# One decoder layer on one core: the time mix part begun inside the last cross attention rounds

## The reference

```python
# 1. self attention with sigmoid instead of softmax
qn, kn = layer_norm(x @ Wq.T + bq), layer_norm(x @ Wk.T + bk)
attn = sigmoid(qn @ kn.T / sqrt(256) - log(1024))
x = layernorm(x + ((attn @ v) @ Wo.T + bo) * layerscale)
# 2. cross attention, 16 heads of 16, over the 77 context tokens
attn = softmax(qh @ kh.T / 4)
x = layernorm(x + (attn @ vh) @ dense_w.T + dense_b)
# 3. time mix (x_prev is x one token earlier in its sequence)
xr, xk = mu_r * x + (1 - mu_r) * x_prev, mu_k * x + (1 - mu_k) * x_prev
out = sigmoid(xr @ W_r.T) * (relu(xk @ W_k.T) ** 2 @ W_v.T)
x = layernorm(x + out)
```

## Time and profile before

| what | value |
|---|---|
| median of three runs | 612.66 us |
| profiled execution, its own time | 616.14 us |
| its span, first to last instruction | 614.3 us |
| mean granted TensorE clock | 0.945 of full speed |
| busy, share of the span: PE / PEld / DVE / ACT / POOL | 88% / 79% / 73% / 76% / 58% |
| ACT_TABLE_LOAD of ScalarE, 1283 ns each | 60 |

### The profile page before, as it was taken

One profiled execution on the slowest core, in us unless ns is written; L12 is line 12 of the kernel. 1 busy time (PEld: TensorE's weight loads), 2 busy tenths in 40 slices (PEclk: granted clock), 3 DMA queues, 4 the chain that ended last, 5 costly groups with the idle time before them and its releaser, 6 DMA issues.

```text
span 614.3 us, 12601 instructions
## 1 busy us (share of the span) xinstructions
PE 537.6 (88%) x4526; PEld 484.4 (79%) x4526; DVE 448.8 (73%) x981; ACT 465.3 (76%) x1109; POOL 358.6 (58%) x498
## 2 busy tenths in 40 slices
PE   7979899899898989898998998898896664699993
PEld 5769898797888879797888887797785444699993
DVE  4775668878779697878788795667664534589995
ACT  2644389797888888887978889988984525799984
POOL 2763547666666575757656664653744531059996
PEclk9999999999999999999999999999997566899998
DMA  6421210101010101101010101102013000001112
GB/s 160 136 72 14 44 35 1 36 1 35 2 53 1 52 2 53 36 19 52 1 37 2 36 1 36 36 1 87 2 37 136 1 2 0 1 18 54 52 52 103
DMA packets 28850, 23.01 MB, mean 37 GB/s; under 512 B 7412, under 2 KB 28788, under 8 KB 28788
## 3 DMA queue, kind: packets, MB, share of 16 engines
q1 hardware_dynamic: 28084, 21.55, 11.5%
q10 hardware_dynamic: 704, 0.66, 0.5%
HBM read 15.07 MB, written 6.82 MB: 36 GB/s over the span
## 4 chain that ended last, share of the span: by engine, by line
PE 30%; DVE 20%; POOL 17%; issue 15%; ACT 13%; DMA 2%; SPq 1%; POOLq 0%; DVEq 0%; ACTq 0%
PE st L257 7%; PE xb L257 6%; POOL p_sb L763 5%; DVE qk_sb L919 5%; PE xb L1366 4%; DVE st L1042 4%; PE proj L257 4%; ACT p_sb L515 4%; PE xb L1350 3%; POOL fold L758 3%; POOL vv_lo L707 2%; POOL xs L751 2%; PE acc L257 2%; POOL rs L698 2%; PE proj L1248 1%
## 5 line engine op out<-in xcount | busy, mean ns | idle before, releaser
L515 ACT ACTIVATE p_sb<-xb,neg_mx 128x77 f32<-128x77 f32 x512 | 114.2, 375 | 19.0 <-DVE neg_mx L981 18.7
L763 POOL TENSOR_TENSOR p_sb<-p_sb,rc 128x1280 f32<-128x1280 f32 x32 | 79.1, 2471 | 74.3 <-DVE rc L994 74.3
L257 PE MATMUL st<-qkT_hi 128*128 128x256 f32 x256 | 76.9, 300 | 0.0
L257 PE MATMUL acc<-vv_hi,aT_hi 128*128 128x256 f32 x256 | 75.3, 294 | 0.0
L257 PE MATMUL st<-qkT_lo,qkT_hi 128*128 128x256 f32 x256 | 72.8, 284 | 0.0
L257 PE MATMUL st<-qkT_hi,qkT_lo 128*128 128x256 f32 x256 | 72.8, 284 | 0.0
L257 PE MATMUL acc<-vv_lo,aT_hi 128*128 128x256 f32 x256 | 72.3, 283 | 0.0
L257 PE MATMUL acc<-vv_hi,aT_lo 128*128 128x256 f32 x256 | 72.3, 283 | 0.0
L1350 PE MATMUL xb<-ident,p_sb 128*128 128x128 f32 x320 | 53.2, 295 | 18.3 <-ACT p_sb L515 13.1
L981 DVE TENSOR_REDUCE neg_mx<-xb 128x4 f32<-128x308 f32 x128 | 52.2, 470 | 18.4 <-PE xb L1337 18.3
L758 POOL TENSOR_TENSOR fold<-p_sb 128x640 f32<-128x640 f32 x32 | 50.7, 1583 | 25.8 <-ACT p_sb L515 25.6
(11 more groups left out here) (201 smaller groups left out, 1750.6 us busy)
## 6 DMA issues: line engine op xcount, KB each, us to landing
xraw<-in_xT SPq DMA_DIRECT2D x16, 256.0 KB, 3.1
xs<-in_x SPq DMA_DIRECT2D x16, 256.0 KB, 3.0
out_y<-y SPq DMA_DIRECT2D x16, 256.0 KB, 2.1
x_kept<-xs SPq DMA_DIRECT2D x10, 256.0 KB, 2.2
x2s<-x_kept SPq DMA_DIRECT2D x5, 512.0 KB, 5.6
cT<-in_cT SPq DMA_DIRECT2D x1, 308.0 KB, 3.3
wraw<-in_wqT ACTq DMA_DIRECT2D x2, 128.0 KB, 3.5
wraw<-in_wkT SPq DMA_DIRECT2D x2, 128.0 KB, 3.7
```

The source lines that it names most:

```text
L257: mm = pe.matmul(out, s_, m_, start=first and k == 0 and q == 0, stop=last and k == n - 1 and q == 2, skip_group_check=not check)
L515: ex = act.activation(weights(t)[:, h // KH * (H // 2) + KH * n + h % KH, 0:SC], logits[n][:, h * SC:(h + 1) * SC], ACT.Exp, bias=neg_mx[: ...
L763: pool.tensor_tensor(weights(t), weights(t), rc[:, t % 2].rearrange("p (h o) -> p h o", o=1) .to_broadcast([P, H, SP]), ALU.mult).then_inc ...
```

## The change

It has five parts.

1. Every engine's order is new. The prologue is written out step by step and reaches further (self attention scores up to number 4 and the first query stand in it); the rounds are 16 with other order inside; everything from there to the end is written out, with steps of the time mix part among the last cross attention steps. `exponentials` and `maxima` are called for one bank of heads at a time, `qk_stats` is cut in `qk_bias` and `qk_stats`, `wf_split` in three.
2. The first five pairs (ND) of the time mix part use the four banks that self attention leaves free; from pair 5 on the banks alternate with those of cross attention.
3. The mixtures are written to SBUF (`xm`) and read there by `mix_hi` and `mix_lo`.
4. The norm of q and k is two tensor_tensor over 512 columns (times scale, then plus bias, both broadcast along the row), the second waiting for the first.
5. The buffers of the time mix part lie where those of the parts before are free earlier; the loads of its weights and of the kept rows are issued earlier.

```diff
-NR_ALL = NJ + 5
+ND = 5
-        xm_bank, fr_bank, fk_bank, fv_bank = st_bank, cross_bank[0], cross_bank[1], [cross_bank[2], cross_bank[3]]
+        def in_turn(own, cross):
+            return lambda i: own if i < ND or (i - ND) % 2 else cross
+        ty_bank, fv_bank = in_turn(proj[:], cross_bank[0]), in_turn(acc_ps[:], cross_bank[2])
+        fr_bank, fk_bank = in_turn(st_bank[0], cross_bank[1]), in_turn(st_bank[1], cross_bank[3])
+        def same_bank(i):
+            return i - 1 if i < ND else i - 2
...
+            xm = tensor(ph, "xm", [P, 2, 2, BANK])
...
             @block.sync
                 def load_again(n):
...
+                    w.wait_ge(*(av_pe.at(4 * (NJ - JB) - 1) if n < JB else st_pe.at(LAST)))
...
-                w.wait_ge(*av_pe.at(LAST))
             @block.scalar
+                    w.wait_ge(*mx_dve.at(t, n + 1))
+                    for h in range(HG):
...
                 def key_relu(i):
                     w.wait_ge(*fk_pe.at(i))
+                    w.wait_ge(*av_pe.at(LAST))
...
+                def round_(r):
+                    at(norm2, r - 5)
+                    at(exponentials, 2 * r - 4, NT, 0, 0)
+                    at(exponentials, 2 * r - 4, NT, 0, 1)
+                    at(exponentials, 2 * r - 4, NT, 0, 2)
+                    at(tqk_hi, 2 * r + 7, NT, 11)
...
+                exponentials(30, 3)
+                weights_tail(29)
+                key_relu(0)
+                carried(2)
+                mixed_hi(14)
+                key_squares(0)
+                exponentials(31, 0)
...
             @block.gpsimd
                 def round_(r):
+                    at(fold_weights, 2 * r - 6, NT)
+                    at(xt_lo, r + 4, NJ, 6)
+                    at(qk_deviation, 2 * r + 6, NT, 11)
+                    at(normalise, 2 * r - 6, NT)
+                    at(deviation1, r - 2, NJ, 1)
+                    at(deviation2, r - 5)
+                    at(fold_weights, 2 * r - 5, NT)
+                    at(residual2, r - 2, NJ, 1)
+                    at(qk_deviation, 2 * r + 7, NT, 11)
+                    at(normalise, 2 * r - 5, NT)
+                    at(v_lo, r + 3, NJ, 6)
+                    at(residual1, r - 1, NJ, 2)
...
             @block.vector
                 def qk_norm(i):
...
+                    both = tiles(qk_sb[:, i % 4])
+                    scale, bias = (t[:, i % 4].rearrange("p (m o) -> p m o", o=1).to_broadcast([P, 2, D]) for t in (rs1, nb1))
+                    dve.tensor_tensor(both, both, scale, ALU.mult).then_inc(qn_dve.sem, 1)
+                    w.wait_ge(*qn_dve.at(i - NF, 1))
+                    dve.tensor_tensor(both, both, bias, ALU.add).then_inc(qn_dve.sem, 1)
...
+                            dve.scalar_tensor_tensor(out=xm[:, i % 2, m, k * D:(k + 1) * D], in0=ty_bank(i)[:, k * D:(k + 1) * D],
...
-                        low_part(hi, lo, xm_bank[m]).then_inc(xml_dve.sem, 1)
+                        low_part(hi, lo, xm[:, i % 2, m]).then_inc(xml_dve.sem, 1)
...
                 def round_(r):
...
+                    at(qk_bias, 2 * r + 7, NT, 14)
+                    at(sums, 2 * r - 5, NT, 2)
+                    at(reciprocals, 2 * r - 5, NT, 1)
+                    at(qk_stats, 2 * r + 7, NT, 14)
+                    at(sigmoid_lo, 4 * r - 1, NS, 10)
+                    at(maxima, 2 * r - 4, NT, 2, 0)
+                    at(qk_norm, 2 * r + 7, NT, 13)
+                    at(maxima, 2 * r - 4, NT, 2, 1)
...
             @block.tensor
                 def round_(r):
-                    at(scores, 4 * r - 1, NS)
-                    at(cross_scores, 2 * r - 5, NT)
-                    at(v, r + 3, NJ, JB)
-                    at(weights_t, 2 * r - 6, NT, 0, 0)
-                    at(scores, 4 * r, NS)
...
+                    at(v, r + 2, NJ, 5)
+                    at(cross_scores, 2 * r - 7, NT)
+                    at(scores, 4 * r - 5, NS, 5)
+                    at(scores, 4 * r - 4, NS, 5)
+                    at(weights_t, 2 * r - 8, NT, 0, 0)
+                    at(weights_t, 2 * r - 8, NT, 0, 1)
...
+                    at(attend, 4 * r - 7, NS, 2)
+                    at(cross_scores, 2 * r - 6, NT)
+                    at(attend, 4 * r - 6, NS, 2)
+                    at(attend, 4 * r - 5, NS, 2)
...
+                cross_scores(30)
+                mix_keys(0)
+                weights_t(29, 0)
+                x2(2)
+                weights_t(29, 1)
+                weights_t(29, 2)
+                mixed(14)
+                receptance(0)
+                cross_scores(31)
+                weights_t(30, 0)
+                mix_values(0)
+                weights_t(30, 1)
+                mix_keys(1)
+                weights_t(30, 2)
+                x2(3)
+                dense(14)
+                receptance(1)
+                weights_t(31, 0)
+                x2(4)
+                weights_t(31, 1)
+                weights_t(31, 2)
+                mix_keys(2)
+                mix_values(1)
+                x2(5)
+                mixed(15)
+                receptance(2)
+                x2(6)
+                mix_keys(3)
+                mix_values(2)
+                receptance(3)
+                dense(15)
+                mix_keys(4)
...
```

More of the change, by code:

```diff
@@ L403, in _ @@
                             sp.dma_start(mu[:, n], io[name]).then_inc(load3.sem, 16)
-                w.wait_ge(*av_pe.at(LAST))
+                    if has(r - 4, NSP):
+                        keep_rows(r - 4)
                 for n in range(NSP // 2):
@@ new lines, in _ @@
+                carried(14)
+                key_squares(12)
+                mix_hi(14)
+                gate_sigmoid(11)
+                key_relu(13)
+                carried(15)
+                key_squares(13)
+                key_relu(14)
+                gate_sigmoid(12)
+                for i in range(5, NJ):
+                    mix_round(i)
+                key_squares(14)
+                mix_hi(15)
+                gate_sigmoid(13)
+                gate_sigmoid(14)
+                norm3(11)
@@ L676, in _ @@
+                key_relu(15)
+                key_squares(15)
+                gate_sigmoid(15)
+                norm3(12)
+                norm3(13)
+                norm3(14)
             @block.gpsimd
@@ new lines, in _ @@
+                key_squares_lo(6)
+                stats3(4)
+                mix_lo(8)
+                mixes(9)
+                key_squares_lo(7)
+                gated(5)
+                mixes(10)
+                mix_lo(9)
+                gated(6)
+                stats3(5)
+                key_squares_lo(8)
+                mix_lo(10)
+                for i in range(5, NJ):
+                    mix_round(i)
+                key_squares_lo(13)
+                gated(12)
+                stats3(11)
@@ L1486, in _ @@
-                x2(0)
-                x2(1)
+                v(4)
+                scores(3)
+                scores(4)
+                tqk(8)
+                attend(0)
+                qk(9)
+                attend(1)
+                for r in range(NJ):
+                    round_(r)
+                weights_t(23, 0)
+                weights_t(23, 1)
+                weights_t(23, 2)
+                scores(57)
+                mixed(11)
+                scores(58)
+                cross_scores(25)
@@ new lines, in _ @@
+                x2(4)
[12 more added lines that the diff above has]
+                mix_keys(4)
+                mix_values(3)
+                x2(7)
+                mix_keys(5)
+                receptance(4)
@@ new lines, in _ @@
+                x2(12)
+                mix_values(8)
+                mix_keys(11)
+                receptance(10)
+                x2(13)
+                mix_values(9)
+                mix_keys(12)
+                x2(14)
+                receptance(11)
+                mix_values(10)
+                mix_values(11)
+                receptance(12)
+                mix_keys(13)
+                x2(15)
+                for i in range(5, NJ):
+                    mix_round(i)
+                mix_values(12)
@@ L1499, in shape_constants @@
+                mix_keys(14)
+                receptance(13)
+                mix_values(13)
+                receptance(14)
+                mix_keys(15)
+                mix_values(14)
+                receptance(15)
+                mix_values(15)
 def shape_constants():
```

940 lines of the change are left out of this document (666 added, 274 removed).

## The result

The changed kernel takes 622.2 us (median of 4 runs, 619.45 to 623.78) beside 612.98 us for the kernel before in the same comparison: a ratio of 1.0136, 95% interval 1.0083 to 1.0189. It is slower by 1.4%, a little but clear of the noise, and outside the forecast range. The profiled execution took 619.45 us with a span of 617.6; that of the kernel before 616.14, span 614.3.

A forecast was written before the change was run, and what follows sets the result against it. TensorE was taken to bound the rounds with projections, one tile's chain the last tiles, four full engines the steady time mix. Terms summed to -25.7 (590.4 beside 616.14), hence 587 us beside 612.66; range 567 to 612, forecast's own 576 to 599.

The forecast's parts named there:

- What bounds the kernel: Rounds with projections: TensorE bounds them, and a new order can take out only the 1.64 us gap a round.
- Prologue: Start of the kernel: five score products fill TensorE's idle time, -3 us, between -7 and +3 (a new stall).
- Rounds with projections: Moved norm still waits for GpSimd, gap about 1.5 us again: -1.5 us in 10 rounds, bounds -16 and +13.
- Rounds without projections: Two score products stand where the 1.71 us gap was, ScalarE late next: -3 us, between -5.7 and +2.
- The last four tiles: Last cross attention tiles: inserted time mix steps fit beside the chain, +3 us, bounds -6 and +18.
- rival B: Last four tiles: the overlap is serial, inserted steps delay the chain, +18 in place of +3, 602 us; chance 0.14.
- What is left after it: After the last dense product: 12.3 pairs at 4.86 us and the end remain, saving 36.6 us.
- the mixtures: Time mix, mixtures in SBUF: mix_lo and GpSimd exclude each other, +1.25 us a pair, +15.4 us, between 0 and +32.
- C: Norm and mix_lo: two-input VectorE instructions wait for GpSimd, +13 in rounds, +32 in mixtures, 618 us; chance 0.16.
- A: Time mix: meetings in SBUF cost next to nothing, +2 in place of +15.4, 569 us; chance 0.14.
- D: Norm in the rounds: slow by its old form, two tensor_tensor are faster, -9 in ten rounds, 578 us; chance 0.06.

The follow-up runs named there:

- e8: Kernel before with GpSimd waiting, in the rounds, for VectorE's norm of tile 2r + 7 ahead of xT_lo: 593.54 us, ratio 0.9705.
- e1_load: Changed kernel with the load of xT for pair 7 moved ahead of SyncE's wait for the zeroed vb: 608.51 us, ratio to before 0.9908.
- e7: Kernel before with only the time mix mixtures written to SBUF instead of two PSUM banks: 623.36 us, ratio 1.0182.
- e4: Changed kernel with one wait added: GpSimd waits for VectorE's norm of tile 2r + 7 ahead of normalise: 593.97 us, ratio to before 0.967.
- e2: Changed kernel with the norm back in its old form, two scalar_tensor_tensor, in its new place: 611.8 us, ratio to before 0.9952.
- e3: Kernel before with only the norm changed to two tensor_tensor, in the old place: 642.54 us, ratio 1.0397.
- e6b: Changed kernel with pair 7's load earlier, GpSimd waiting for the norm, score products ahead of weights_t, norm as two scalar_tensor_tensor: 571.24 us, ratio to before 0.9306.

## Why the prediction was wrong

*What bounds the kernel*: right as far as it went. The claim that the 1.64 us gap is all that a new order can take out of the rounds is confirmed by e8 (28.1 to 26.22). But it was read as the most that could change, and a gap that grows was priced at its own length.

*Prologue, -3 (-7 to +3)*: the step that failed first, +10.3 against it. The step reasoned about TensorE's slices and five score products. It named neither `value_zeros`, which was moved behind `residual2(0)`, nor SyncE's wait on it. With the zeroing later, the wait holds the 24 small transfers, and these hold `load_xt(7)`. The bound of +3 for "a new stall" had no row under it. e1_load gives the size: 13.7 us. Without the stall pair 1 is 2.1 us earlier than before, so the -3 itself was near.

*Rounds with projections, -1.5 (-16 to +13)*: the larger failure, +21.7 with the round behind them. The mechanism was right to a few tenths: the prediction had 4.8 us for waiting and norm (measured 4.47, from 266.28 to 270.75), 5.3 with the maximum in front (5.5), and 3.1 of cover (3.1, from 265.12 to 268.2). 5.3 - 3.1 = 2.2, and the measured gap is 2.55. Then it took 0.7 off, for a norm that could be late to normalise's start. The trace has the opposite: the norm also waits 0.55 us for GpSimd's `nb`, normalise has started 0.08 us ahead of it, and nothing comes off. The second and heavier miss is not in the sum at all: behind a gap of 2.0 to 2.6 us the granted clock falls, 1.5 to 1.7 us a round. Over the nine rounds from pair 1 to pair 10 the ledger has +18.3. Without this term the upper bound of 1.3 us a round was no bound; 2.6 came in the full rounds.

*Rounds without projections, -3*: -4.2 over four rounds, right in sign, with some luck in the size. The kernel of e7, which is that of before up to the time mix part, has 91.17 us from pair 11 to pair 15 where the trace of before has 93.54; against that the changed kernel's 89.39 is -1.8.

*The last four tiles, +3*: +4.1, right, at clock 0.99 in place of 0.63. The insertion works beside the chain, and rival B (serial, +18) is false. TensorE has no wait there for a kept row's load.

*What is left after it, -36.6, and the mixtures, +15.4*: together -21.2 forecast, -28.6 measured. 13 value products were left, as counted, the first at 541.72 and the last at 609.02: 67.3 / 12 = 5.6 us a pair, where the prediction had 4.86 + 1.25 = 6.1. So the term of the mixtures was sized too high; 12.3 x 0.75 = 9 us, or 11.3 by e7; `mix_lo` took 0.96 us on average, where 1.0 to 1.5 had been forecast. The mechanism stands: pairs of low parts at 1.28 us alone and up to 2.4 with GpSimd, though in the rows above it was `residual3` that they met and not the halves of `norm3`. Here the miss helped the change.

*The rivals.* C had the place and the sign, at 618 against 622: VectorE's two-input instructions waiting for GpSimd. Its own split was wrong, though: +13 in the rounds and +32 in the mixtures, where the ledger and e7 have about +22 and +9 to +11. Some 14 of the 22 came through the clock, which C does not have, and the late load hides in neither; that its sum is near 622 is luck. In what it cites from the Trainium skill, SBUF — State Buffer, SBUF: two separate sides, the exclusive lock for the whole instruction, the runs agree: 0.69 us a tensor_tensor when GpSimd waits (e4), 2.80 and 1.63 when it does not. A (the meetings cost nothing) is false by e4 and e7. D (slow by its form) is false by e2 and e3; with it the rule of the Trainium skill, Vector Engine (DVE) Microarchitecture Reference, Points that are easy to get wrong, that two fp32 sources in SBUF halve the throughput of a scalar_tensor_tensor, finds no support here: at 256 columns one with both in SBUF takes 0.48 us, the same as the mixtures' with one in PSUM, and replacing the form made the kernel before 4% slower.

What stays open: why the clock fell behind most gaps of 2.01 us in e2 and not behind two of them (nor behind one of 2.17 us in the changed kernel, at 150.14, and one in e3); where the 6 us lie by which the medians differ more than the two traces; and what else moving `value_zeros` back alone would have done. A version with e8's rounds (26.22 us against e6b's 27.00) and the changed kernel's tail was not tried, and neither was a wait like e4's in the time mix part, for the meetings that e7 prices.

## What to carry to other kernels

When a step moves, list who waits for it on every queue, SyncE's first, and everything behind that wait: a memset that was free where it stood cost some 13.7 us, by e1_load and the estimate above, through the load queued behind it. Look at an instruction's shortest and longest time when both its inputs are in SBUF; if they differ by a factor of three, look at GpSimd in the same microseconds, and let GpSimd wait for the few hundred nanoseconds that VectorE needs, if it has time to spare (-28 and -18.5 us here for one line). Price a gap of TensorE with the clock behind it, not by its length alone.

## What was not expected of the hardware

- Short gaps inside a busy stretch lowered the granted clock. Behind 2.55 us idle it was 0.67 for 5.1 us, behind 2.17 us 0.66 for 5.0 in most rounds and 1.00 in two (e3 at 363.89, the changed kernel at 150.14), behind 2.01 us 0.65 or 0.70 in most and 1.00 in two; behind 1.64 and 1.48 us it was 1.00. So the length of the gap alone does not decide it.
- Two VectorE instructions in a row each waited for a GpSimd instruction of their own: GpSimd's next one came in between them. 2.80 + 1.63 us against 0.69 + 0.69; as two scalar_tensor_tensor 3.93 us against 0.87.
- Whoever came second paid. GpSimd's normalise, which started first, took 2.33 us both with VectorE queued against it and with VectorE's norm kept out of its way; but its next instruction, the low part of v, met the first tensor_tensor and took 1.71 us instead of the 1.29 of e4_poolwait.
- The 24 small transfers from `v` into `vb` (3 to 19 KB each) took 21.63 us of SyncE's queue to issue, 0.90 us each. It is not their size alone: the issue of `xs` at 96.79 (256 KB) took 0.46 us, and that of `bqcol` (1 KB) 0.47 in the same queue.
